# Binary layer on one core: 64x64 weight tiles, sums of signs 512 wide, gates spread through DRAM

## The reference

```python
gate = bin_gate(sigmoid(x @ proj_w.T + proj_b))   # 8 gates per token, 0 or 1
w    = einsum('hbe,heio->hbio', gate, weight)     # a 64x64 weight matrix per token
y    = einsum('hbi,hbio->hbo', sign(x), sign(w))
h    = h + y * scale
```

## Time and profile before

| | |
|---|---|
| median of 3 executions | 1733.34 us (1732.08 to 1734.09) |
| profiled execution, its own time | 1728.17 us |
| its span | 1726.4 us |
| mean granted clock of PE | 0.978 |
| PE busy | 1590.4 us (92%) |
| PEld busy | 1205.7 us (70%) |
| DVE busy | 1205.9 us (70%) |
| ACT busy | 969.9 us (56%) |
| POOL busy | 539.3 us (31%) |

### The profile page before, as it was taken

One profiled execution on the slowest core, in us unless ns is written; L12 is line 12 of the kernel. 1 busy time (PEld: TensorE's weight loads), 2 busy tenths in 40 slices (PEclk: granted clock), 3 DMA queues, 4 the chain that ended last, 5 costly groups with the idle time before them and its releaser, 6 DMA issues.

```text
span 1726.4 us, 87999 instructions
## 1 busy us (share of the span) xinstructions
PE 1590.4 (92%) x32618; PEld 1205.7 (70%) x32618; DVE 1205.9 (70%) x3509; ACT 969.9 (56%) x1893; POOL 539.3 (31%) x699
## 2 busy tenths in 40 slices
PE   6898998779999999999996799999999999999996
PEld 4666676557888888888875566766666676666663
DVE  3887878746666666666654777787788778778762
ACT  1333333244444444444432477888888788888867
POOL 3311111054555555555541221222222222222210
PEclk9999999969999999999997899999999999999998
DMA  5101010034444444444431233333333333333332
...
DMA packets 134691, 143.29 MB, mean 83 GB/s; under 512 B 42498, under 2 KB 90114, under 8 KB 134370
## 3 DMA queue, kind: packets, MB, share of 16 engines
...
## 4 chain that ended last, share of the span: by engine, by line
PE 81%; DVE 6%; issue 5%; SPq 3%; ACT 3%; DMA 1%; POOL 1%; DVEq 0%; ACTq 0%; POOLq 0%
PE ps_D L888 11%; PE ps_D L799 8%; PE ps_OT L818 4%; PE ps_J L838 4%; PE ps_D L676 3%; PE ps_AV L824 3%; PE ps_AV L905 3%; SPq L463 3%; PE ps_D L795 3%; PE ps_J L760 2%; PE ps_OT L752 2%; DVE tile_a L1286 2%; PE ps_J L996 2%; ACT prob L1176 2%; PE ps_J L964 2%
## 5 line engine op out<-in xcount | busy, mean ns | idle before, releaser
L1176 ACT ACTIVATE prob<-ps_D 128x1024 bf16<-128x1024 f32 x448 | 459.4, 1029 | 123.7 <-PE ps_D L888 122.1
L1146 ACT ACTIVATE prob<-ps_D 100x512 f32<-100x512 f32 x256 | 138.8, 594 | 219.2 <-PE ps_D L799 219.2
L1350 DVE TENSOR_REDUCE m_sb<-ps_D 128x4 f32<-128x400 f32 x256 | 135.4, 570 | 90.1 <-PE ps_D L776 90.0
L799 PE MATMUL ps_D<-tile_a,key_patch 64*100 64x128 f32 x2048 | 173.3, 287 | 0.6 <-issue 0.6
L888 PE MATMUL ps_D<-tile_b,w_parts 128*128 128x256 bf16 x1024 | 150.8, 272 | 14.2 <-DVE xg L1472 4.5
L888 PE MATMUL ps_D<-tile_a,w_parts 128*128 128x256 bf16 x1024 | 153.2, 276 | 9.5 <-ACT prob L1176 3.0
L799 PEld LDWEIGHTS ps_D<-tile_a,key_patch 64*100 64x100 f32 x2048 | 135.3, 165 | 0.8 <-issue 0.8
L553 POOL TENSOR_TENSOR tile_a<-q_st,q_mask 128x1024 f32<-128x1024 f32 x64 | 123.4, 1928 | 22.3 <-PE ps_D L799 10.6
L528 POOL TENSOR_TENSOR rstd_bin<-veps_bin,minus_half 128x2 f32<-128x2 f32 x64 | 44.1, 688 | 269.4 <-DVE veps_bin L1237 269.4
L795 PE MATMUL ps_D<-mT,key_rows 64*100 64x128 bf16 x1024 | 121.0, 226 | 7.8 <-issue 7.4
L528 POOL TENSOR_TENSOR rstd_ret<-veps_ret,minus_half 128x2 f32<-128x2 f32 x64 | 46.5, 727 | 250.8 <-DVE veps_ret L1237 250.8
...
## 6 DMA issues: line engine op xcount, KB each, us to landing
tile_a<-xg SPq DMA_DIRECT2D x384, 64.0 KB, 2.0
tile_b<-xg SPq DMA_DIRECT2D x384, 64.0 KB, 2.0
key_st<-k_d SPq DMA_DIRECT2D x128, 162.0 KB, 3.1
tile_b<-v_d ACTq DMA_DIRECT2D x128, 120.0 KB
...
xT<-in_x SPq DMA_DIRECT2D x32, 256.0 KB, 2.7
k_d<-kpad SPq DMA_DIRECT2D x64, 64.0 KB, 2.9
```

Source lines behind the costliest of these rows:

```text
L799: mm = pe.matmul(s_loc[x][0:NKL, u * P:(u + 1) * P], key_patch[rows_of(x), par, at * NKL:(at + 1) * NKL], q_block[rows_of(x), par, at * P: ...
L1146: act.activation(prob1[0:NKL, 2 * g + x, :], s_loc[x][0:NKL, :], ACT.Exp).then_inc(T2["exp_done"], 1)
L1176: act.activation(sgn[:, k % 4, :], unit(k, par)[:, :], ACT.Sign).then_inc(BN["sign"], 1)
L1350: dve.tensor_reduce(m_sb[:, C * x + HOT[x] + 4 * g:C * x + HOT[x] + 4 * g + 4], m_loc[x][:, 0:4 * NKL].rearrange("p (u n) -> p u n", u=4), ...
```

## The change

It does five things.

- A weight unit is now 8 matmuls with weights of 64 x 64 over the same 256 tokens. The input rows are split in halves (x) and so are the output rows (lanes); the four combinations lie on four quarters of PE's array and write to different halves of the partitions and different banks. Rows 0 to 47 and 64 to 111 of the buffer hold data, 3 parts of 16 rows in each half.
- The sums of a pair of units are 4 matmuls over 512 columns instead of 8 over 256, into all 512 columns of bank AV. `ysum` is 512 wide, and the fold has 4 matmuls instead of 2, which accumulate in pairs.
- The copies of `xg` go through a DRAM tensor `x_d`: two stores of 64 rows x 3 copies x 2 KB, then, when these have landed, two loads of 48 rows x 8 KB. The wait for the weight units of two strips before now stands between stores and loads. DVE waits for the stores (`x_out`) before it overwrites `xg`; PE waits for the loads (`x_in0`, `x_in1`).
- POOL zeroes four blocks of 32 rows instead of two, and SP waits for them before its part of the last stage.
- The weights' parts are made over 128 rows, and placed by two multiplications and four multiply-adds (steps 2 to 4) instead of three copies and four multiplications over 96 rows.

```diff
@@ -108,11 +113,12 @@
-    group, lane, gate = np.arange(P) // 32, np.arange(P) % 32 // NG, np.arange(P) % NG
-    t["lane_mask"] = (lane[:, None] == np.arange(4)[None, :]).astype(np.float32)
+    half, part, lane = np.arange(P) // 64, np.arange(P) % 64 // 16, np.arange(P) % 16 // NG
+    t["part_mask"] = ((part[:, None, None] == np.arange(3)[None, :, None]) & (lane[:, None, None] == np.arange(2)[None, None, :])).astype(np.float32).reshape(P, 6)
+    group, line = np.arange(P) % 4, gate_line() // NG
-        spread[C + 16 * n + 4 * group + lane, n, np.arange(P)] = 1
+        spread[C + 32 * half + 2 * (4 * group + n) + line, n, np.arange(P)] = 1
@@ -155,7 +161,7 @@
-        w_parts, lane_mask = sb("w_parts", [P, 16, 2, 4, 32], BF16), sb("lane_mask", [P, 4])
+        w_parts, part_mask = sb("w_parts", [P, 16, 2, 2, 32], BF16), sb("part_mask", [P, 6])
@@ -192,14 +198,14 @@
-        PARTS = 96
-        w_bin, w_rest = key_patch[0:PARTS, :, :].rearrange("p a n -> p (a n)")[:, 0:1024], key_rows[0:PARTS, :, :].rearrange("p a n -> p (a n)")[:, 0:1024]
-        w_high, w_mid, w_sel = rot[0:PARTS, 0, :].bitcast(BF16), rot[0:PARTS, 1, :].bitcast(BF16), q_sb[0:PARTS, :, :].rearrange("p a n -> p (a n)").bitcast(BF16)
-        ysum, ys, yo = sb("ysum", [P, 256], BF16), sb("ys", [P, 2, C]), sb("yo", [P, 2, C])
+        w_bin, w_rest = key_patch[:, :, :].rearrange("p a n -> p (a n)")[:, 0:1024], key_rows[:, :, :].rearrange("p a n -> p (a n)")[:, 0:1024]
+        w_high, w_mid, w_low = rot[:, 0, :].bitcast(BF16), rot[:, 1, :].bitcast(BF16), q_sb[:, :, :].rearrange("p a n -> p (a n)").bitcast(BF16)
+        ysum, ys, yo = sb("ysum", [P, 512], BF16), sb("ys", [P, 2, C]), sb("yo", [P, 2, C])
+        x_d = nc.dram_tensor("x_d", (NSTRIP, 2, 3, 16, 4, 1024), BF16, kind="Internal").ap()
@@ -457,10 +463,15 @@
 
             def spread_in(g, par):
                 sp.wait_ge(BN["xg"], times(g + 1))
+                for half in range(2):
+                    sp.dma_start(x_d[bass.ds(g, 1), half, :, :, :, :].rearrange("a p l g n -> (a l g) p n"),
+                                 xg[rows_of(half), :].rearrange("r (p n) -> r p n", p=1).broadcast_to((C, 3, 1024))).then_inc(BN["x_out"], 16)
                 sp.wait_ge(BN["w_ps"], times((g - 1) * 8))
-                for part in range(3):
-                    for n in range(4):
-                        sp.dma_start(x_parts[par][32 * part:32 * (part + 1), 1024 * n:1024 * (n + 1)], xg[32 * n:32 * (n + 1), :]).then_inc(BN["x_in"], 16)
+                sp.wait_ge(BN["x_out"], times((g + 1) * 32))
+                settle(sp)
+                for half in range(2):
+                    sp.dma_start(x_parts[par][C * half:C * half + 48, :],
+                                 x_d[bass.ds(g, 1), half, :, :, :, :].rearrange("a p l g n -> (a p l) (g n)")).then_inc(BN["x_in%d" % par], 16)
 
             def strips(j, par):
                 if not isinstance(j, int) or j < NS:
@@ -473,6 +484,7 @@
+            sp.wait_ge(s_clear, 4)
@@ -582,10 +594,11 @@
-            gp.memset(tile_a[PARTS:P, :, :], 0.0).then_inc(s_clear, 1)
-            gp.wait_ge(s_clear, 1)
-            gp.memset(tile_b[PARTS:P, :, :], 0.0).then_inc(s_clear, 1)
-            gp.wait_ge(s_clear, 2)
+            for n, (tile, at) in enumerate(((tile_a, 32), (tile_a, 96), (tile_b, 32), (tile_b, 96))):
+                if n:
+                    gp.wait_ge(s_clear, n)
+                gp.memset(tile[at:at + 32, :, :], 0.0).then_inc(s_clear, 1)
+            gp.wait_ge(s_clear, 4)
@@ -883,10 +896,12 @@
                 def weights(k, half, d):
                     settle(pe)
                     for oh in range(2):
-                        for a in range(2):
-                            at = (2 * (k % 2) + a) * 4 + k // 2
-                            mm = pe.matmul(d[:, a * 512 + oh * 256:a * 512 + (oh + 1) * 256], w_parts[:, at, oh, :, :].rearrange("r i o -> r (i o)"),
-                                           x_parts[half][:, at * 256:(at + 1) * 256], start=True, stop=True)
+                        for lanes in range(2):
+                            for x in range(2):
+                                at = 2 * k + lanes
+                                mm = pe.matmul(d[rows_of(lanes), x * 512 + oh * 256:x * 512 + (oh + 1) * 256],
+                                               w_parts[rows_of(x), at, oh, :, :].rearrange("r i o -> r (i o)"),
+                                               x_parts[half][rows_of(x), at * 256:(at + 1) * 256], start=True, stop=True)
                     mm.then_inc(BN["w_ps"], 1)
 
                 def signed(q, k):
@@ -901,9 +916,10 @@
                     signed(q, 2 * pair + 1)
                     settle(pe)
                     for k in (2 * pair, 2 * pair + 1):
-                        for cg in range(4):
-                            mm = pe.matmul(bank["AV"][32 * cg:32 * (cg + 1), 0:256], lane_sum[:, int(k == 1), :], sgn[:, k % 4, cg * 256:(cg + 1) * 256],
-                                           start=k == 0, stop=k == 7)
+                        for oh in range(2):
+                            cg = 2 * (k % 2) + oh
+                            mm = pe.matmul(bank["AV"][32 * cg:32 * (cg + 1), :].rearrange("o (x t) -> o x t", x=2), lane_sum[:, int(k == 1), :],
+                                           sgn[:, k % 4, :].rearrange("r (x h t) -> r h x t", x=2, h=2)[:, oh, :, :], start=k < 2, stop=k >= 6)
                     mm.then_inc(BN["y_part"], 1)
 
                 if q is not None:
@@ -983,7 +999,9 @@
-                        mm = pe.matmul(bank["T"][:, 256 + t * C:256 + (t + 1) * C], ysum[:, t * P:(t + 1) * P], half_sum[:, :], start=True, stop=True)
+                        for x in range(2):
+                            mm = pe.matmul(bank["T"][:, 256 + t * C:256 + (t + 1) * C], ysum[:, 256 * x + t * P:256 * x + (t + 1) * P], half_sum[:, :],
+                                           start=x == 0, stop=x == 1)
@@ -1041,8 +1059,8 @@
-                        pe.wait_ge(s_clear, 2)
-                    pe.wait_ge(BN["x_in"], times((n + 1) * 192))
+                        pe.wait_ge(s_clear, 4)
+                    pe.wait_ge(BN["x_in%d" % (1 - par)], times((n + 1 + par) * 16))
@@ -1180,7 +1198,7 @@
-                    act.activation(ysum[:, :], bank["AV"][:, 0:256], ACT.Copy).then_inc(BN["ysum"], 1)
+                    act.activation(ysum[:, :], bank["AV"][:, :], ACT.Copy).then_inc(BN["ysum"], 1)
@@ -1414,17 +1432,18 @@
                 if j == 1:
                     dve.wait_ge(s_placed, 5)
                     dve.tensor_copy(w_mid, w_rest).then_inc(s_placed, 1)
-                    dve.tensor_copy(w_sel[0:32, :], w_high[0:32, :]).then_inc(s_placed, 1)
-                if j == 2:
-                    dve.wait_ge(s_placed, 7)
-                    dve.tensor_tensor(w_sel[64:96, :], w_rest[64:96, :], w_mid[64:96, :], ALU.subtract).then_inc(s_placed, 1)
-                    dve.tensor_copy(w_sel[32:64, :], w_mid[32:64, :]).then_inc(s_placed, 1)
-                if j == 3:
-                    dve.wait_ge(s_placed, 9)
-                if j in (3, 4):
-                    for lane in (2 * j - 6, 2 * j - 5):
-                        dve.tensor_scalar(w_parts[0:PARTS, :, :, lane, :], w_sel.rearrange("p (n h o) -> p n h o", n=16, h=2),
-                                          lane_mask[0:PARTS, lane:lane + 1], None, ALU.mult).then_inc(s_placed, 1)
+                    dve.wait_ge(s_placed, 6)
+                    dve.tensor_tensor(w_low, w_rest, w_mid, ALU.subtract).then_inc(s_placed, 1)
+                if j in (2, 3, 4):
+                    for lane in range(2):
+                        dve.wait_ge(s_placed, 7 + 2 * (j - 2) + lane)
+                        dst = w_parts[:, :, :, lane, :]
+                        src = (w_high, w_mid, w_low)[j - 2].rearrange("p (n h o) -> p n h o", n=16, h=2)
+                        own = part_mask[:, 2 * (j - 2) + lane:2 * (j - 2) + lane + 1]
+                        if j == 2:
+                            dve.tensor_scalar(dst, src, own, None, ALU.mult).then_inc(s_placed, 1)
+                        else:
+                            dve.scalar_tensor_tensor(out=dst, in0=src, scalar=own, in1=dst, op0=ALU.mult, op1=ALU.add).then_inc(s_placed, 1)
 
             def strips(j, par):
                 e, f, r, b, g, q, p = (inside(j - k) for k in (0, 1, 2, 3, 4, 6, 7))
@@ -1468,7 +1487,7 @@
-                    dve.wait_ge(BN["x_in"], times(g * 192))
+                    dve.wait_ge(BN["x_out"], times(g * 32))
@@ -1546,9 +1565,9 @@
-    arr["w_gate"] = np.pad(np.tile(n(L1_ffn_proj_w).T, (1, P // NG)), ((C, 0), (0, 0)))
-    arr["b_gate"] = np.tile(n(L1_ffn_proj_b), P // NG).reshape(P, 1)
-    arr["w_bin"] = np.tile(n(L1_ffn_weight)[0].reshape(NG, 4, 4, 4, C).transpose(3, 0, 2, 1, 4).reshape(32, -1), (3, 1))
+    arr["w_gate"] = np.pad(n(L1_ffn_proj_w).T[:, gate_line() % NG], ((C, 0), (0, 0)))
+    arr["b_gate"] = n(L1_ffn_proj_b)[gate_line() % NG].reshape(P, 1)
```

(1 more changed line is left out.)

6 lines of the change are left out of this document (4 added, 2 removed).

## The result

The changed kernel takes **1757.6 us** (median of 4 executions, 1756.1 to 1761.3) against 1732.7 for the kernel before, run beside it: 1.0158 times as long, 95% interval 1.0142 to 1.0175 (the two medians alone divide to 1.0144). The prediction was 1703, range 1685 to 1738. It missed the sign.

What follows compares the result with a forecast made beforehand. PE's chain was taken to bound the last stage's step: -0.55 us (11.61 to 11.06) over 64 steps gives -35, the stage's start +5.4, total -30, so 1703 us against the median 1733.3; range 1685 to 1738.

Steps and rivals of the forecast that it cites:

- Each leg: 2.0 + 704 KB / 274 GB/s = 4.6 us ... It is hidden, with 1.8 us to spare.: Stores to and loads from DRAM: 4.6 us each, round trip 10.6 us against 12.4 allowed, costing the step nothing.
- the round trip is late: DRAM stores and loads: legs of 7.1 us at half the rate make the step 12.65, 1805 us; chance 0.15.
- if the step is above 11.4, or if PE's wait ahead of unit 0 is released by `x_d`: Signs in the new trace of the last stage that would show the forecast wrong; it expected a step of 11.06 us.
- The units: Weight products on PE: four array quarters run at once, 0.24 us per unit, saving 0.20 each.
- two at a time: Weight products on PE: a unit stays at 0.44 us, step about +0.6, 1777 us; chance 0.14, including worse.
- slow weight loads: Weight products on PE: plain loads of 53 ns, eight in a row, make a unit 0.43 us; no separate chance.
- The changes of shape: PE's switches between 64x64 units and neighbouring blocks: eight new ones per step, 0.10 us each.
- the 0.35 given for no drain: PE's shape switches: if changing tiling drained nothing, the step sum would be an estimated 0.35 us better.
- the rival's -0.9: PE's shape switches cost nothing, loads overlapping the old block: -0.9 us per step, 1681 us; chance 0.11 with cheap sums.
- hidden behind the clip: Unit 2 and the transposes on PE lie behind DVE's clip of unit 1, so are off the step's chain.
- ACT's wide copy: ACT's copy of the sums, now 512 columns: 0.59 instead of 0.38 us, making the first expert matmul some 0.09 late.
- The fold's +0.06: The fold on PE: two more matmuls of 64 columns add 0.06 us per step.

Runs made afterwards that it cites:

- narrow_sums: one_store with the sums of signs, their copy and the fold put back to the 256-wide form of the kernel before; 1707.4 us, 0.986 of the kernel before.
- one_store: Changed kernel with one store of 128 rows without copies, its two loads reading every DRAM row three times; 1725.9 us, 0.998 of the kernel before.
- filled_wait: Changed kernel with 256-wide sums, copy and fold, plus eight overwritten 64x64 matmuls before PE's wait for the load; 1765.5 us, 1.019 of the kernel before.

## Why the prediction was wrong

Per step: forecast -0.55, measured +0.28 (11.64 to 11.92). The runs split it into three terms: the units alone -0.40 (narrow_sums against before; forecast -0.70, which is -0.55 less the 0.06 and 0.09 for fold and copy), the wide sums +0.23 (one_store against narrow_sums; forecast +0.15), the transfers +0.45 (the changed kernel against one_store; forecast 0).

- **The step that failed: "Each leg: 2.0 + 704 KB / 274 GB/s = 4.6 us ... It is hidden, with 1.8 us to spare."** The legs took 5.45 and 7.65, and the round trip was not hidden: 0.45 us per step instead of 0. The rate of 274 GB/s came from two other kinds of transfer, a copy of 64 KB between rows of SBUF and a load of 256 KB, and I did not ask how the new transfers are cut up. The halves of 64 and 48 rows were in the diff. The Trainium skill (SBUF — State Buffer, Door 1: The DMA port swizzle) says that the rows of one half of the partitions reach only half of SBUF's ports. By that rule the two stores have half the width each, and the trace fits it: 5.45 us for them, 3.56 for the same bytes from all rows. No run here separates the number of rows from the way the copies are made, for the stores, or from the number of transfers, for the loads (7.4 us for two of 48 rows, 5.3 for one of 96). So that the legs were late and cost 0.45 is shown; why they were is in part argued.
- **The rival "the round trip is late" was the right mechanism**, with a chance of 0.15. Its formula holds: with the terms of this trace (14.27 + 9.59) / 2 = 11.93, for a step that took 11.92 on average. It was priced for legs of 7.1 each, 15.6 in all; 14.3 to 14.6 came. The forecast said wrong "if the step is above 11.4, or if PE's wait ahead of unit 0 is released by `x_d`". Both happened.
- **The units: right.** 0.24 beside a like one, 0.34 with a change behind, as forecast: eight matmuls of 0.11 each in 0.24, so four quarters do run at once. The rivals of two at a time and of slow weight loads fell.
- **The changes of shape: a term too small.** Counted were eight of 0.10. Units 4 and 7 stand ahead of float32 blocks and cost 0.10 more each, 0.20 per step. (The shape terms on the chain add up to 0.50 in the sum, so the 0.35 given for no drain, and the rival's -0.9 with it, do not follow from it.) Another 0.07 or so was missing between unit 1 and the first expert matmul: there PE also waits for the sign of unit 0 ahead of unit 2, which the prediction held to be hidden behind the clip. That wait (14.7 us in 45 times in narrow_sums) is the longest that PE has left there.
- **ACT's wide copy: right in kind, 0.08 too low.** It was to be "some 0.09 late", where the terms beside it (0.58 less 0.40, 0.21 and 0.1) give 0.13; PE waits 0.26 us per step for `xs` behind it, and the wide sums cost 0.17 beyond the fold. The fold's +0.06 is right (L1003 to unit 5 is 0.21, in narrow_sums 0.15).
- **Wide sums bring nothing by themselves: right.**
- **The start: a little short.** 7.9 us from the first memset to the first unit against 5.4 forecast. Another 2.9 us lie ahead of the stage. That beginning differs between 923 and 933 us among all these runs and is not the change's.
- **The other signs.** `xg` waits for no transfer any more, as forecast (PE L1024 ends its wait). ACT is busy for 79 of 100 us and not for 83, and the clock is 0.98 in that stretch and not 1.00; filled_wait has the same transfers and the same step at a clock of 1.00, so the clock is not what made the changed kernel slow.

Over the 64 steps the 0.86 us by which 11.92 exceeds 11.06 are 55 us. The profiled execution was forecast at 1698 and took 1756.1, 58 us more: these 55, 2.5 at the start and 2.9 ahead of the stage, less some 2, since the kernel before has 11.64 by this measure and not 11.61.
